# ScalarE normalises the rows of the four LayerNorms with a scale and a bias column that VectorE makes; another order on all engines

## What is computed

```python
def _layernorm(x, axis=-1, eps=1e-05):
    m = jnp.mean(x, axis=axis, keepdims=True)
    v = jnp.var(x, axis=axis, keepdims=True)
    return (x - m) / jnp.sqrt(v + eps)
...
h = _L0_tok_ref(x, ...)            # depthwise 3x3 convolution, 8x8 mean
h = h + _L0_attn_ref(_layernorm(h), ...)   # one head of 128, over 64 tokens
h = h + _L0_ffn_ref(_layernorm(h), ...)    # 2 shared experts, 8 routed (top 2)
h = h + _L1_attn_ref(_layernorm(h), ...)   # 8 heads, rope, also over 15 means of 8 tokens
h = h + _L1_ffn_ref(_layernorm(h), ...)    # two lower triangular 128x128 layers, gelu between
```

## Time and profile before

| | us |
|---|---|
| median of three runs | 1983.51 |
| lowest, highest | 1963.71, 1990.41 |
| profiled execution | 2000.31 |
| its span, first to last instruction | 1998.4 |
| mean granted clock in it | 0.932 |

### The profile page before, as it was taken

One profiled execution on the slowest core, in us unless ns is written; L12 is line 12 of the kernel. 1 busy time (PEld: TensorE's weight loads), 2 busy tenths in 40 slices (PEclk: granted clock), 3 DMA queues, 4 the chain that ended last, 5 costly groups with the idle time before them and its releaser, 6 DMA issues.

```text
span 1998.4 us, 42920 instructions
## 1 busy us (share of the span) xinstructions
PE 1700.6 (85%) x14896; PEld 1320.4 (66%) x14896; DVE 1307.9 (65%) x3244; ACT 1070.4 (54%) x2707; POOL 754.4 (38%) x643
## 2 busy tenths in 40 slices
PE   1453888989998989999899999898999999897947
PEld 1443666867677777778676777777776768575624
DVE  2467476878677777568686777777777868442222
ACT  0122545647474747466564747474757566553532
POOL 1324244352536263344525263626353434213020
PEclk9999989999899999799998999999999999988775
DMA  6547455555655554445555555555455543101000
GB/s 253 223 172 261 164 209 194 184 176 183 219 182 176 202 203 173 153 174 191 181 187 206 183 196 205 176 186 206 163 208 185 203 164 147 43 15 53 12 22 6
DMA packets 109125, 331.56 MB, mean 166 GB/s; under 512 B 13662, under 2 KB 87585, under 8 KB 92412
## 3 DMA queue, kind: packets, MB, share of 16 engines
q1 hardware_dynamic: 86416, 300.90, 41.5%
q0 software_dynamic: 8992, 19.42, 3.0%
q10 hardware_dynamic: 13516, 8.50, 1.4%
HBM read 299.48 MB, written 29.29 MB: 165 GB/s over the span
## 4 chain that ended last, share of the span: by engine, by line
PE 42%; POOL 19%; DVE 14%; issue 13%; ACT 6%; DMA 4%; ACTq 1%; another core or an unknown queue 0%; SPq 0%; POOLq 0%; DVEq 0%
PE hid_bank L595 7%; POOL yg L1374 7%; PE sec_bank L649 5%; POOL rows_d L1352 5%; PE pool_bank L449 3%; POOL xbuf L1363 3%; PE sec_bank L669 3%; PE sec_bank L660 3%; PE hid_bank L580 3%; PE hid_bank L579 3%; PE pool_bank L454 2%; DVE xc L1268 2%; POOL rs L1335 2%; DVE x L1055 2%; PE hid_bank L581 2%
## 5 line engine op out<-in xcount | busy, mean ns | idle before, releaser
L1363 POOL TENSOR_TENSOR xbuf<-xbuf 128x512 f32<-128x512 f32 x256 | 328.2, 1282 | 633.0 <-DVE xbuf L1063 621.7
L845 ACT ACTIVATE hid<-hid_bank,bias_t 128x128 f32<-128x128 f32 x960 | 273.1, 371 | 116.0 <-PE hid_bank L581 113.6
L595 PE MATMUL hid_bank<-w_s,hid 128*128 x1920 | 291.2, 297 | 0.0
L595 PEld LDWEIGHTS hid_bank<-w_s,hid 128*128 128x128 f32 x1920 | 244.4, 199 | 16.9
L1084 DVE SCALAR_TENSOR_TENSOR taps<-pooled_s,tapw,taps 128x256 f32<-128x256 f32 (+1 forms) x416 | 240.5, 578 | 10.6
L1063 DVE TENSOR_TENSOR xbuf<-xbuf 128x1536 f32<-128x1536 f32 x128 | 224.0, 1750 | 30.4 <-DMA xbuf<-in_x 30.3
L579 PE MATMUL hid_bank<-xt,w_b 128*128 128x128 bf16 x960 | 213.2, 234 | 35.0 <-issue 17.1
L580 PE MATMUL hid_bank<-xt,w_b 128*128 128x128 bf16 x960 | 213.5, 234 | 0.7
L581 PE MATMUL hid_bank<-xt,w_b 128*128 128x128 bf16 x960 | 209.5, 230 | 0.0
L1374 POOL DMA_INDIRECT yg<-outs_d,spot_i x128 | 151.2, 1182 | 54.7 <-issue 38.8
L1067 DVE TENSOR_TENSOR xbuf<-xbuf 128x512 bf16<-128x512 f32 x128 | 102.1, 797 | 98.4 <-ACT xbuf L759 94.6
(11 more groups left out here) (215 smaller groups left out, 3464.8 us busy)
## 6 DMA issues: line engine op xcount, KB each, us to landing
xbuf<-in_x SPq DMA_DIRECT2D x128, 2048.0 KB
...
rows_d<-x2r,spot_i POOLq DMA_INDIRECT x128
yg<-outs_d,spot_i POOLq DMA_INDIRECT x128
```

The source lines that it names most:

```text
L595: mm = nc.tensor.matmul(hid_bank[n % 2][:, 0:P], hid[:, n % RING, q * P:(q + 1) * P], w_q, start=False, stop=q == FC - 1)
L845: ins = nc.scalar.activation(hid[:, n % RING, cols], hid_bank[n % 2][:, cols], ACT.Gelu, bias=bias_t[:, q, j:j + 1])
L1363: nc.gpsimd.tensor_tensor(v[:, :, 1, :], v[:, :, 1, :], v[:, :, 2 * k + 3, :], ALU.add) \
```

## The change

DVE's four instructions per LayerNorm become one: nb = -mean * rs, a [128 x 4] tile (`centre`). ACT gets four new pieces, norm1 to norm4, each with four Identity activations: rs * x + nb, with both as column operands. All five lists of `ORDER` are new; in them norm1 to norm4 are placed on ACT, and old pieces have changed places on every engine.

```diff
-                att="att", low="att", high="att", rest="att", scatter="att", up="ffn", hidden="ffn", down="ffn", moe="ffn",
+                att="att", low="att", high="att", norm1="att", norm2="att", norm3="sec", norm4="sec", rest="att", scatter="att", up="ffn", hidden="ffn", down="ffn", moe="ffn",
...
     pe="""
...
-        pool.0.1 down.6 down.7 pool.0.2 lift.0 att.1 lift.1 widen.0 lift.2 widen.1 att.2 narrow.0 lift.3 pool.0.3
...
+        down.7 pool.0.0 lift.0 pool.0.1 widen.0 lift.1 pool.0.2 lift.2 att.1 narrow.0 att.2 widen.1 lift.3 att.3
...
+        value.2 widen.9 turn.4 value.3 pool.2.3 lift.11 att.10 turn.5 lift.12 value.4 att.11 turn.6 value.5
+        narrow.9 widen.10 lift.13 turn.7 value.6 att.12 narrow.10 widen.11 pool.3.0 value.7 widen.12 pool.3.1
+        post.0 narrow.11 post.1 widen.13 narrow.12 lift.14 pool.3.2 narrow.13 widen.14 pool.3.3 post.3 narrow.14
...
+        nb1, nb2, nb3, nb4 = sb("nb1", [P, T]), sb("nb2", [P, T]), sb("nb3", [P, T]), sb("nb4", [P, T])
...
+            def normalise(g, dst, src, nb, rs, centred, ready):
+
+                eng.wait_ge(centred, at(centred, g, 1))
+                for t in range(T):
+                    nc.scalar.activation(dst[:, t, :], src[:, t, :], ACT.Identity, bias=nb[:, t:t + 1],
+                                         scale=rs[:, t:t + 1]).then_inc(ready, 1)
+
             def attention(g, b, n):
                 bank = att_bank
-                if n == 1:
+                if n == "norm1":
+                    if after(g, 1):
+                        eng.wait_ge(o1_done, at(o1_done, g - 1, 1))
+                    normalise(g, x1, h0[b], nb1, rs1, centred1, x1_ready)
+                elif n == "norm2":
+                    normalise(g, x2, h1[b], nb2, rs2, centred2, x2_ready)
...
+                if kind == "norm3":
+                    normalise(g, x3, h2, nb3, rs3, centred3, x3_ready)
+                elif kind == "norm4":
+                    normalise(g, x3, h3, nb4, rs4, centred4, x4_ready)
...
-            def normalise(g, dst, src, mv, rs, rstd, ready, read=None, need=0):
+            def centre(g, nb, mv, rs, rstd, centred):
                 eng.wait_ge(rstd, at(rstd, g, 1))
-                if read is not None and after(g, 1):
-                    eng.wait_ge(read, at(read, g - 1, need))
-                for t in range(T):
-                    nc.vector.tensor_scalar(dst[:, t, :], src[:, t, :], mv[:, t, 0:1], rs[:, t:t + 1],
-                                            ALU.subtract, ALU.mult).then_inc(ready, 1)
+                nc.vector.scalar_tensor_tensor(nb[:], mv[:, :, 0], -1.0, rs[:], ALU.mult, ALU.mult).then_inc(centred, 1)
```

More of the change, by code:

```diff
@@ L58 @@
     sp="""
[L59 to L61 removed]
+        store.8' store.10' store.11' load.0.0 store.9' store.12' store.13' load.0.1 store.14' rows.0 rows.1
+        load.1.0 load.1.1 store.2 load.2.0 load.2.1 store.0 store.3 store.4 rows.2 store.1 load.3.0 store.6
+        store.5 store.7 load.3.1 keep.0""",
@@ L62 @@
     pe="""
-        up.0 up.1 table up.2 up.3 down.0 down.1 down.2 up.4 down.3 up.5 out' up.6 down.4 down.5 up.7 pool.0.0
-        pool.0.1 down.6 down.7 pool.0.2 lift.0 att.1 lift.1 widen.0 lift.2 widen.1 att.2 narrow.0 lift.3 pool.0.3
-        lift.4 widen.2 pre.2 narrow.1 pre.3 lift.5 att.3 lift.6 narrow.2 pre.4 att.4 pre.5 pre.6 lift.7 pre.7
-        widen.3 pool.1.0 pool.1.1 widen.4 pool.1.2 score.0 score.1 att.7 score.2 score.3 narrow.3 score.4
-        pool.1.3 score.5 widen.5 narrow.4 score.6 score.7 lift.8 att.8 widen.6 narrow.5 turn.0 widen.7 turn.1
@@ L68 @@
-        pool.2.0 lift.9 value.0 pool.2.1 narrow.6 turn.2 lift.10 pool.2.2 att.10 widen.8 value.1 turn.3 value.2
-        narrow.7 turn.4 pool.2.3 value.3 lift.11 widen.9 turn.5 value.4 narrow.8 turn.6 value.5 att.11 widen.10
-        turn.7 lift.12 narrow.9 value.6 narrow.10 value.7 widen.11 att.12 lift.13 post.0 widen.12 pool.3.0 post.1
-        narrow.11 pool.3.1 pool.3.2 narrow.12 lift.14 widen.13 widen.14 pool.3.3 narrow.13 post.3 narrow.14
+        up.0 table up.1 up.2 down.0 up.3 down.1 up.4 up.5 out' down.2 down.3 up.6 up.7 down.4 down.5 down.6
@@ new lines @@
+        down.7 pool.0.0 lift.0 pool.0.1 widen.0 lift.1 pool.0.2 lift.2 att.1 narrow.0 att.2 widen.1 lift.3 att.3
+        pool.0.3 narrow.1 att.4 pre.2 lift.4 widen.2 pre.3 narrow.2 lift.5 pre.4 widen.3 pre.6 widen.4 lift.6
+        pool.1.0 pool.1.1 narrow.3 pre.5 pool.1.2 lift.7 pre.7 lift.8 widen.5 score.0 score.1 narrow.4 score.2
+        pool.1.3 score.3 widen.6 score.4 att.7 score.5 lift.9 narrow.5 score.6 score.7 narrow.6 att.8 pool.2.0
+        pool.2.1 widen.7 turn.0 widen.8 turn.1 pool.2.2 value.0 lift.10 narrow.7 turn.2 value.1 narrow.8 turn.3
@@ L76 @@
-        widen.2 lift.5 narrow.1 att.3 lift.6 gate narrow.2 pre.5 inner.1.0 pre.6 pre.7 split att.6 widen.3
-        inner.1.1 pool.1.0 pool.1.2 widen.4 narrow.3 att.7 pool.1.3 lift.7 widen.5 narrow.4 exp lift.8 narrow.5
-        inner.2.0 turn.0 widen.6 lift.9 turn.1 narrow.6 turn.2 widen.7 high att.10 lift.10 inner.2.1 turn.3
-        pool.2.0 pool.2.2 narrow.7 widen.8 turn.4 turn.5 widen.9 pool.2.3 narrow.8 turn.6 lift.11 widen.10 turn.7
-        narrow.9 inner.3.0 lift.12 narrow.10 widen.11 post.0 widen.12 narrow.11 pool.3.0 lift.13 pool.3.2
@@ L92 @@
[L92 to L97 removed]
+        hidden.0 table hidden.1 hidden.2 hidden.3 out' hidden.4 hidden.5 hidden.6 inner.0.0 hidden.7 lift.0 norm1
@@ new lines @@
+        lift.1 widen.0 att.1 inner.0.1 lift.2 att.2 pool.0.0 widen.1 att.3 pool.0.2 norm3 pool.0.3 narrow.0
+        lift.3 pre.2 widen.2 lift.4 narrow.1 narrow.2 inner.1.0 lift.5 widen.3 pre.6 split lift.6 pre.5 lift.7
+        narrow.3 pre.7 widen.4 pool.1.0 inner.1.1 pool.1.2 att.6 pool.1.3 gate narrow.4 widen.5 lift.8 att.7
+        widen.6 inner.2.0 narrow.5 exp lift.9 narrow.6 pool.2.0 turn.0 widen.7 turn.1 lift.10 widen.8 inner.2.1
+        turn.2 pool.2.2 narrow.7 turn.3 norm2 turn.4 high lift.11 att.10 turn.5 widen.9 lift.12 narrow.8 turn.6
```

53 lines of the change are left out of this document (26 added, 27 removed).

## The result

The changed kernel is slower, outside the forecast range. The median of four runs is 2055.05 us (2050.25 to 2082.38), beside 1976.32 us of the kernel before; the ratio is 1.0388, with a 95% interval from 1.0284 to 1.0493. The ratio is of the fast executions alone and the medians are of all, so that the two need not divide exactly. Forecast were 1973 us. The profiled execution took 2050.25 us; its span is 2048.5 us, 50 us more than before.

A forecast was written before the change was run, and what follows sets the result against it. PE was taken to bound the kernel, at 107.9 us per iteration. -2.6 - 0.8 + 2.4 = -1.0 us, times fourteen -14, with the ends -10: 2000.3 becomes 1990, or 1973 us on the median's scale; range 1935 to 2008.

The forecast's parts named there:

- The change part by part: The prediction's costing of the change, engine by engine and place by place, summing to -1.0 us per full iteration.
- Rival B: First lift still waits, inner.0.0 hanging on add.0.1 behind five gathers: +1.5 us per iteration, 2008 us; chance 0.15.
- The clock: From 20 to 32 us of an iteration, behind the wait at lift.0: 0.8 us per iteration saved (0 to 1.55).
- The prediction's own sign of being wrong: The prediction is wrong if PE waits for ACT at widen or score by over 2 us per iteration.
- The wait at lift for `moe`: Start of the iteration: with moe ahead of att.1 on DVE, 1.7 us per iteration of PE's wait go.
- The wait at `up`: A down between up.2 and up.3 takes the smaller gelu wait: 0.4 us per iteration saved (0 to 0.6).
- New waits at value.6 and post.0: At the gate, value.5 and value.7 now stand behind att.11 and att.12 on DVE: 0.7 and 0.8 us lost.
- Rival A: Clean start, clock included, no new waits as PE reaches value.6 and post.0 late anyway: 1929 us; chance 0.2.
- norm1, norm2 and norm3 find their columns about ready: 0: On ACT, these three norms find their columns about ready when ACT comes to them: 0 us lost.
- ACT's Identity: Each of sixteen Identity instructions with two column operands takes 462 ns, bounds 371 and 524.
- The column on DVE: Each [128x4] column on DVE priced as L1048, 164 ns; four of them 0.7 us per iteration.
- The ends: First two iterations +1 us (0 to 1.4); last two, where nothing covers the chain, four LayerNorms of 0.7: +2.8.

The follow-up runs named there:

- e1: The changed kernel with store.14' put back ahead of load.0.1 in SP's list: 1977.76 us, 0.998 of the kernel before.
- e4: The kernel before with one exchange, load.0.1 ahead of store.14', nothing normalised on ACT: 2043.93 us, 1.032 of the kernel before.
- e21: The changed kernel itself, measured again in another group: 2058.39 us, 1.042 of the kernel before.
- e22: The program of e1 measured again, in the group of e21: 1968.47 us, 0.997 of the kernel before.
- e19: The changed kernel with store.14' ahead of load.0.1, but the 2 MB load.0.0 moved right ahead of store.14': 2052.77 us, 1.038 of the kernel before.
- e23: The changed kernel's lists without norm1 to norm4, DVE normalising as before, store.14' ahead of load.0.1: 1949.45 us, 0.984 of the kernel before.

## Why the prediction was wrong

**The step that failed.** "The change part by part" costs PE, DVE, ACT and POOL, and never SP. The new SP list, among other changes, puts load.0.1 ahead of store.14', and the prediction had no term for it. e1, e4, e21 with e22, and e19 show what it costs: 3.2 to 4.5%, 63 to 90 us.

**Rival B** named the place (the pieces at the first lift hang on inner.0.0, which hangs on add.0.1 behind five gathers) and gave it an estimated slack of 0.5 us and a price of +1.5 us per iteration. The price assumed that gather.0 starts when it did before. It starts 6.9 us late, which no slack there holds. The chance of 0.15 was for a smaller thing.

**The clock.** The prediction let it gain 0.8 us per iteration. It lost 2.9: behind the one stall of 3.8 us PE was granted 0.50 to 0.65 where it had 0.72 to 1.00, and with the stall gone (e1) the twelve iterations have 0.96. The place was right; that the idle time ahead of it would shrink was not. The prediction's own sign of being wrong was a wait for ACT of over 2 us at widen or score. PE did wait for ACT by more than that, but at down.7.

**The rest of the sum**, read from e1, where only the store is put back: 106.5 us per iteration (1278.3 / 12), 1.4 less than before; forecast were 1.0 less. By its terms:
- The wait at lift for `moe`, 1.7 us per iteration: gone, as forecast.
- The wait at `up`: 14.4 us to 4.8, 0.8 per iteration where 0.4 were forecast.
- New waits at value.6 and post.0, 0.7 and 0.8: not there. No row of the changed kernel or of e1 shows PE waiting for DVE in the twelve iterations. Rival A had supposed that PE comes there later than my sum of starts; no run tests why.
- "norm1, norm2 and norm3 find their columns about ready: 0": wrong for norm1. It waits for its column, and the copy of lift.1 behind it holds lift.2 for 27.5 us, 2.3 per iteration. POOL's power behind the gathers and the column's 1.23 us under POOL's adds are both rows that I had used for DVE's old instructions and not for the new one.
- ACT's Identity: 462 ns forecast, measured a median of 483 and a mean of 497 (x1, x3, x4), inside the bounds. The column on DVE: 164 ns forecast, 427 on average, which hides two values: in each of the twelve iterations norm1's takes 1.23 to 1.25 us and the other three 0.15 or 0.16.
- The ends, +1 and +2.8: e1 against e23 is 0.2 us longer up to the twelve iterations and 2.7 after them (both read at the first matmul of up.1).
- Split in two, the sum had -27 us for the lists (-2.6 - 0.8 + 1.5, times 14) and +17 for the move (0.9 x 14 + 4). Measured in the undisturbed groups are -1.6% (e23), -32 us, and +26 us. That the lists' total came near is luck: the two new waits of 1.5 us per iteration did not come, one at att.1 of 2.1 (25.2 / 12) came instead, and PE's work shrank by 1.9 ((1214.7 - 1191.8) / 12), where 0.8 were forecast for the clock. The part left out was larger than all of them.

The column's and the Identity's rows, changed kernel, twelve iterations (busy us, mean ns | idle before):

```profile
L787 ACT ACTIVATE x<-h,nb,rs 128x128 f32<-128x128 f32 x144 | 59.6, 497 | 24.5 <-DVE nb L1072 24.5
...
L1072 DVE SCALAR_TENSOR_TENSOR nb<-mv,rs 128x4 f32<-128x4 f32 x48 | 20.5, 427 | 41.1 <-POOL rs L1351 41.1
```
